# Two-layer conditioned transformer on one core: last element's stacks in layer 0's buffers, K's first half stacked ahead of Q's second, first statistics ahead of the modulation, new order tables

## The reference, cut to what matters

```python
# layer 0 (D = 256, H = 16 heads of 16)
mod = silu(cond) @ Wada + bada
sh_a, sc_a, gt_a, sh_m, sc_m, gt_m = split(mod, 6)
xm = layernorm(x, g1, be1) * (1 + sc_a) + sh_a
x  = x + gt_a * causal_attention(xm, Wqkv, Wproj, bproj)
xm = layernorm(x, g2, be2) * (1 + sc_m) + sh_m
x  = x + gt_m * (gelu(xm @ W1 + b1) @ W2 + b2)
# layer 1 (not causal; its MLP weights are not used)
h  = gamma(cond) * ln(x) + beta(cond)
q, k, v = split(h @ Wqkv1.T + bqkv1)
out = (softmax(q @ k.T) / 16) @ v
h1 = out @ Wp1.T + bp1 + x
return gamma(cond) * ln(h1) + beta(cond) + h1
```

## Time and profile before

| | us |
|---|---|
| median of 3 runs | 1286.21 (1285.28 to 1287.02) |
| the profiled execution | 1288.15 |
| its span, first to last instruction | 1286.4 |
| PE busy | 1198.2 |
| DVE busy | 858.4 |
| ACT busy | 688.6 |
| POOL busy | 273.5 |
| mean granted TensorE clock | 0.969 of 2.4 GHz |

### The profile page before, as it was taken

One profiled execution on the slowest core, in us unless ns is written; L12 is line 12 of the kernel. 1 busy time (PEld: TensorE's weight loads), 2 busy tenths in 40 slices (PEclk: granted clock), 3 DMA queues, 4 the chain that ended last, 5 costly groups with the idle time before them and its releaser, 6 DMA issues.

```text
span 1286.4 us, 18823 instructions
## 1 busy us (share of the span) xinstructions
PE 1198.2 (93%) x6604; PEld 593.7 (46%) x6604; DVE 858.4 (67%) x1779; ACT 688.6 (54%) x1356; POOL 273.5 (21%) x378
## 2 busy tenths in 40 slices
PE   6897999999999999999999999999999999999796
PEld 4434553455344644546344544446345543444223
DVE  4744478835888378855887469865797468833765
ACT  1152245465555565575555665575555666456173
POOL 1123022401133113321133113320233103220002
PEclk9789999999999999999999999999999999999698
DMA  4603022400513023410414014410414014200401
GB/s 159 199 2 99 1 67 67 125 19 18 150 37 123 2 84 85 120 39 18 128 49 134 1 63 106 105 55 19 118 56 129 2 40 104 53 26 12 105 19 42
DMA packets 59191, 89.36 MB, mean 69 GB/s; under 512 B 12914, under 2 KB 23762, under 8 KB 59098
## 3 DMA queue, kind: packets, MB, share of 16 engines
q1 hardware_dynamic: 58078, 87.35, 24.1%
q10 hardware_dynamic: 1020, 0.81, 0.2%
HBM read 24.41 MB, written 4.70 MB: 23 GB/s over the span
## 4 chain that ended last, share of the span: by engine, by line
PE 69%; ACT 9%; SPq 8%; DVE 7%; issue 3%; DMA 3%; POOL 1%; ACTq 0%; DVEq 0%; POOLq 0%
PE X L1019 17%; PE OP L927 12%; PE SC L938 10%; PE X L957 10%; PE X L1068 8%; PE X L1044 8%; ACT E L607 7%; SPq L484 6%; DVE MX L747 3%; PE X L1032 2%; DMA OC<-OE 2%; PE X L960 1%; SPq L421 1%; PE X L1097 1%; DVE XN L797 1%
## 5 line engine op out<-in xcount | busy, mean ns | idle before, releaser
L747 DVE TENSOR_REDUCE MX<-X 128x1 f32<-128x512 f32 (+3 forms) x1024 | 535.9, 585 | 182.2 <-PE X L960 111.7
L607 ACT ACTIVATE E<-SC 128x512 f32<-128x512 f32 (+3 forms) x1024 | 455.9, 527 | 340.4 <-PE SC L938 278.3
L957 PE MATMUL X<-KS,QS 96*128 96x512 bf16 (+3 forms) x1024 | 309.4, 353 | 22.6 <-DMA KS<-PART 8.9
L938 PE MATMUL SC<-QS,KS 99*128 99x512 bf16 (+3 forms) x1024 | 284.0, 347 | 21.7 <-ACT E L607 12.0
L927 PE MATMUL OP<-E,V 128*32 128x512 f32 (+3 forms) x2048 | 212.9, 533 | 4.2 <-ACT OE L622 3.1
L938 PEld LDWEIGHTS SC<-QS,KS 99*128 99x128 bf16 x1024 | 95.4, 98 | 192.0 <-ACT E L607 116.8
L957 PEld LDWEIGHTS X<-KS,QS 96*128 96x128 bf16 x1024 | 98.6, 99 | 175.3 <-DVE MX L747 59.8
L525 POOL TENSOR_SCALAR_AFFINE_SELECT E<-E 128x512 f32<-128x512 f32 x128 | 83.6, 656 | 266.7 <-ACT E L607 266.7
L1068 PE MATMUL X<-XT,W 128*128 128x512 f32 x256 | 121.9, 607 | 3.3 <-ACT XT L640 2.7
L1044 PE MATMUL X<-XT,WQKV 128*128 128x512 f32 x256 | 118.2, 605 | 1.0 <-ACT XT L640 1.0
L1019 PE MATMUL X<-W,HID 128*128 128x256 f32 x512 | 115.6, 381 | 0.5 <-ACT HID L660 0.5
(11 more groups left out here) (92 smaller groups left out, 944.0 us busy)
## 6 DMA issues: line engine op xcount, KB each, us to landing
QS<-PART SPq DMA_DIRECT2D x192, 128.0 KB, 2.3
KS<-PART SPq DMA_DIRECT2D x192, 128.0 KB, 2.4
OC<-OE SPq DMA_DIRECT2D x56, 128.0 KB, 3.8
RB<-recip_sums SPq DMA_DIRECT2D x56, 128.0 KB, 2.6
XIN<-in_x SPq DMA_DIRECT2D x8, 512.0 KB, 4.1
ROW<-row_vectors SPq DMA_DIRECT2D x8, 512.0 KB, 3.5
out<-OUT SPq DMA_DIRECT2D x7, 512.0 KB, 3.0
W<-in_w SPq DMA_DIRECT2D x2, 1024.0 KB, 7.4
```

The costliest lines, as they stand in the source:

```text
L607: a.activation(E[:, at["tick"].index() % 3, j, lo:T], SC[(at["head"].index() + j) % 3][:, lo:T], ACT.Exp, scale=HD ** -0.5 if layer == 0 e ...
L747: v.reduce_max(MX[:, qt, h:h + 1], X[at["bank"].index() % BANKS][:, 0:w], AX.X, negate=True)\
L938: t_.matmul(SC[(at["head"].index() + j) % 3][:, lo:T], KS[layer][0:ALL_ROWS, h, kt * P:kt * P + P], QS[layer][0:ALL_ROWS, h, lo:T], start= ...
L957: ins = t_.matmul(bank[:, 0:w], QS[layer][0:CUT_ROWS, h, qt * P:qt * P + P], KS[layer][0:CUT_ROWS, h, 0:w], start=True, stop=layer == 1)
```

## The change

Four edits:

- The last element's layer 1 is stacked in QS[0] and KS[0] (function `stacks`). Its stacks no longer wait for layer 1's attention of the element before but for all of layer 0's last attention (`4 * STEPS * (2 * B - 2)` exponentials). Scores, scans and the maxima's rows follow.
- A stack is issued in halves: stackq sends Q's first half (6 DMAs); stackk sends K's first half, then Q's second, then K's second.
- On DVE the first modulation (`first_modulation`) moves from ahead of the lists to inside norm_a of element 0, so behind stat_a.
- The three lists are written in another order, with the same tokens.

```diff
+def stacks(layer, b):
+    return 0 if (layer, b) == (1, B - 1) else layer
...
+            def stack(side, n, half, ready):
+                rows = slice(P // 2 * half, P // 2 * half + P // 2)
+                heads = slice(H // 2 * half, H // 2 * half + H // 2)
+                parts = (Q_PARTS, K_PARTS)[side]
+                for part in range(3):
+                    wait(sp, (high_act, cut_low, cut_low)[part], ready[part])
+                    for r in range(CUTS):
+                        if parts[r] == part:
+                            sp.dma_start((QS, KS)[side][n][r:CUT_ROWS:CUTS, heads, :],
+                                         PART[rows, side, part, :, :]).then_inc(stack_dma[n][half], 16)
...
-                    n, side = int(what[-1]), "qk".index(what[5])
+                    n, side = stacks(int(what[-1]), b), "qk".index(what[5])
                     if side == 0:
-                        wait(sp, exp_done, at["head"].at())
-                    for half in range(2):
...
+                        wait(sp, exp_done, 4 * STEPS * (2 * B - 2) if n < int(what[-1]) else at["head"].at())
+                        marks["stackq"] = marks[what[5:]]
+                        stack(0, n, 0, marks[what[5:]])
+                    else:
+                        stack(1, n, 0, marks[what[5:]])
+                        stack(0, n, 1, marks["stackq"])
+                        stack(1, n, 1, marks[what[5:]])
...
+                    if what == "norm_a" and b == 0:
+                        first_modulation()
...
-                    wait(pe, stack_dma[layer][h // (H // 2)], 192 * (b + 1))
+                    wait(pe, stack_dma[stacks(layer, b)][h // (H // 2)], 192 * (b + 1 + layer - stacks(layer, b)))
...
-    stat_a norm_a turn_a q0 stackq0 k0 mods stackk0 rows s s s s v0 s s s s s s s s s s s s s s s s s nm0_0 s s
+    stat_a norm_a turn_a q0 stackq0 k0 stackk0 mods rows s v0 s s s s s s s s s s s s s s s s s s s s s s s s s
...
-    a p a o p a p turn_1 o a t p q1 a o p a p k1 stackq1 stackk1 o v1 s s s s s s s s s s s s s s s s s s nm1_0
+    a q1 t k1 p a p stackq1 stackk1 a p a o s s p s s a s s s o s t s p s s a s p s s s a s nm1_0 p s s o row1 s
```

96 lines of the change are left out of this document (44 added, 52 removed).

## The result

| | before | after |
|---|---|---|
| median of the runs, us | 1285.99 | 1252.05 |
| lowest and highest | 1285.28 to 1287.02 | 1248.17 to 1255.32 |
| profiled execution (its span) | 1288.15 (1286.4) | 1251.06 (1249.3) |

The ratio is 0.974, with a 95% interval of 0.972 to 0.976: 34 us faster, where 16.7 were forecast.

A forecast was written before the change was run, and what follows sets the result against it. PE was taken as full mid-program, so only the late stretch and the start count: 10.8 us (last element) plus 5.9 us (opening and a wait near 203 us) make 16.7, so 1286.21 becomes 1269.5 us; range 1257 to 1284.

The forecast's parts named there:

- Part 1: Last passes: stacking the last element in layer 0's buffers, with an order that uses it, gains 10.8 us, 4 to 16.
- (a): Between turn_1's transposes and k1's end: three attention steps and two product pairs no longer stand there, 6.3 us gained.
- (b): Ahead of turn_1 in the last passes: five steps and one product pair are gone, 4 us taken, between 1 and 6.2.
- (c): From last k1's end to the last 16 steps: 26.5 us become about 24, set by ScalarE's strand; 2.5 us gained.
- the latency strand: After last k1: cuts, K's first-half DMAs, 16 maxima, then the first score; 21.2 us, shorter than ScalarE's about 24.
- (d): Among the last steps: v1's 16 matmuls now stand there and cost 3.7 us, or 0 if PE has holes.
- (e): After the late hole: the clock falls less with attention steps running through, 2 us back, 0 to 3.
- the rival in which it isn't early: Last element: SP's queue or the exponential count still holds the last stacks back, only 5.9 us left, 1280 us; chance 0.04.
- Part 2: Program start: the first statistics ahead of the modulation bring XN to 10.2 us, 2.9 us earlier, never more than 3.2.
- Part 3: Opening: K's first half ahead of Q's second gives 1.3 us at the first scan; 2.1 us near 203 us.
- Part 4: Five repeated passes in the new order: 0 us, from -1 to +2, though ten fewer table loads could give 12.8.
- VectorE ahead of turn_1: Repeated passes: seven moved maxima delay XN, each pass loses 4.2 us, 1290.5 us in all; chance 0.11.

The follow-up runs named there:

- p1: The kernel before with only the last element's layer 1 stacked in layer 0's buffers and the new order of the last passes; 1272.05 us, ratio 0.988.
- e3: The changed kernel with the old order of the opening passes put back; 1266.89 us, ratio 0.986.
- e5: The changed kernel with the new opening order only up to element 0's merge, the old opening order from there on; 1261.88 us, ratio 0.981.
- e9: The changed kernel with the old order of the repeated pass put back; 1254.76 us, ratio 0.974.
- e12: The changed kernel with the new opening order only up to just ahead of the third element's q0, the rest in old order; 1263.16 us, ratio 0.983.
- p2: The kernel before with only the first statistics put ahead of the first modulation; 1285.28 us, ratio 0.999.
- e6: The changed kernel with the first modulation again ahead of the first statistics; 1257.22 us, ratio 0.979.
- p3: The kernel before with only the stacks issued by halves, all orders old; 1280.67 us, ratio 0.997.
- e7: The changed kernel with whole stacks again, 12 DMAs of Q and then 12 of K; 1264.29 us, ratio 0.982.
- e10: The kernel before with the exponentials between element 1's eight gelus moved out, four table loads fewer; 1287.57 us, ratio 1.001.

## Why the prediction was wrong, point by point

**The direction was right, and the two places that were costed gave about what was forecast. The sum was half, because what lay between them was put at nothing.** In the order of its steps:

*Part 1, the last element: right, a little small.* 10.8 forecast; S6 gives 13.1, and 11.4 with part 1 alone. By its terms, from the Q stack that starts S6 to k1's end 135.3 us became 123.4, so (a) and (b) are 11.9 for 10. From k1's end to the first of the last 16 steps 26.5 became 25.6, so (c) is 0.9 for 2.5, and it was costed on the wrong strand. ScalarE's, my 24 us, holds only 16.8 us of work in the 25.6 (and its terms add up to 22.4 to 22.9, not to 24). What lasted was the latency strand, 21.2 in the prediction: 8.2 us to the first scan where 6.4 were counted (K's first half is issued after 5.1 us and not 4.0, and PE is in a product with V until 8.2), 10.5 from there to the end of the 16th maximum, and 6.9 to the first score where 5.2 were, with one more product with V just ahead of it. From there to the end 70.55 became 70.26, so (d) and (e) are +0.3 for -1.7. Either v1's 3.6 us fit into PE's idle time, which is 14.7 us there before and 14.1 after, or the clock, 0.91 before and 0.95 after, gave back more than the 2 counted; no run parts the two. The early stack is real: Q's DMAs start at 1150.79 with eight steps of the element before still to come, so the rival in which it isn't early is dead. The 13.1 is rather low. In e3, e5, e9 and e12, which run the same instructions there, S6 is 216.2 to 217.0 us with the clock at 0.98, against 219.3 and 0.96.

How big the prize could be was weighed with the Trainium skill ("Perfetto Trace Analysis", Identifying the Most-Contended Engine, on weight loads as the better measure than matmul busy time). The 7.2 us of the earlier trace rows and the 13.1 of S6 don't test this: the first is PE's idle time in one stretch of 32 us, and in all of S6 it was 30.6 us and became 21.5. The hole itself gave little, 11.9 us of the 13.1 lie ahead of k1's end. The trace agrees with the page in S5: PE's busy time falls by 12.0 us between e9 and the kernel after, while the weight loads' stays, at 356.3 and 356.8, and so does the time, at 726.4 and 726.0.

Two side sums of the prediction are off, and nothing rests on them. The prediction's 1275 with 7.2 as the whole prize doesn't come out by putting 7.2 for the 10.8, which gives 1273.1; it takes v1's 3.7 and the clock's 2 on top. And ScalarE's 39 us of the 52 in the last steps leave 13, not 12.

*Part 2, the statistics: right.* XN at 9.95 for 10.2, S1 2.5 to 4.3 us shorter for 2.9 (p2 and after against e6).

*Part 3, the halves: right in place, small in one term, and 2.1 us too large in another.* First scan 31.90 for 32.5, maxima from 37.47 for 38.5, v0 not slowed. The first score is at 53.58 instead of 58.65, 5.1 us earlier for 3.8. The wait for K's stack in S4 is gone, as forecast, but it was not worth its 2.1 us: with the halves and the old order S4 is 137.0 to 137.6, with the wait 137.6 to 139.7, 138.3 in the kernel before. The halves' value at the end, 3.5 us by p3 and e7, was inside the reckoning of (c).

*What followed the opening: the step that failed.* The prediction took the first list as two places: the opening, worth 3.8 us, and "one more place, near 203 us, where PE waits 2.1 us for K's stack". Everything else between the first score, at 58.65 us, and the end of S4, at 323.58, was put at nothing. The traces show 5.1 us gained by the first score and 19.5 by the end of S4, so 14.5 us where 2.1 were counted: 4.9 in what is left of S2, 2.4 in S3 and 7.2 in S4. The list's 461 tokens run to 324 us, and the order of all that stands behind element 0's merge was changed too. I costed it at that one wait because the stretch of the earlier trace rows at 544 us has PE at 32.00 of 32, and I took what holds for the repeated pass for the passes ahead of it. A busy row of 185 to 324 us would have shown 6.8 us idle of 138 and the four kinds of waits.

What is shown of the cause differs by stretch. In S4 it is the order, worth 6 to 7 us (e5, and all 17 kernels of the table). S3 is 2 to 4 us shorter in most kernels with the new order, but part of its work has moved ahead of the mark; e5 keeps S3 at 79.4 with the old order behind the merge. S2's 4.9 go for the most part with the clock, as told below. By which mechanism the order shortens S4 is open: not the table loads (e10), not the wait for K's stack. The 7.2 us are 3.8 of idle time and 3.4 of shorter rows of PE, but S5 shows that the time need not follow either: there 12.0 us of rows and 16 us of waits change with the order, and the time stands.

*The clock: counted as 2 us, about 8 go with it.* Each run comes with its mean granted clock. Within the runs of one kernel, 171 runs in 20 groups, each taken against its group's mean, 0.01 of clock goes with 9.0 us (standard error 0.5). The kernel before has 0.974 (68 runs), the one after 0.983 (4 runs): 0.009 x 900 = 8 us. Most of it lies in S2 (0.83 before, 0.91 after) and S6 (0.93 and 0.96). These 8 us are no addition to the stretches, they are a part of them, and they are a correlation: no kernel here set the clock alone, and which brings the other is not shown.

*Part 4, the repeated pass: right.* 0 forecast, 145.2 us a pass where 146.1 were, and e9, with 145.3, gives no sign that even this is the order's. The table loads, from 51 to 41, are worth nothing, in e9 as in e10. VectorE ahead of turn_1 didn't become the bound. The low end of the range was drawn from those table loads, the one thing in the change that is worth nothing, so it was short by 5 us for a reason that had nothing to do with the loads.

**S2 stays partly open.** Its length goes with its clock. p1 has the instructions of the kernel before there. The rows of S2 in the kernel before, in p1 and in the kernel after:

```profile
22.76:103.21 80.45, 70.83 (x435) 35.80 (x433) 44.16 (x106) 30.27 (x77) 19.25 (x35) 0.83 0.32 100
```

```profile
23.45:99.69 76.24, 65.92 (x435) 35.31 (x433) 43.36 (x106) 29.83 (x77) 19.25 (x35) 0.91 0.33 105
```

```profile
19.66:93.25 73.59, 64.38 (x443) 34.34 (x441) 42.80 (x106) 30.44 (x77) 16.84 (x34) 0.91 0.35 109
```

So of the 6.9 us some 4.2 go with the clock and are within what chance does to the same instructions, and 2.6 are left for the edits at the same clock, with eight matmuls more in them. The new order with the halves has 73.6 to 73.9 at 0.91 (four kernels) and 77.0 and 77.1 at 0.87 (e6 and e5), the new order with whole stacks 79.6 at 0.87 and 82.8 at 0.84, and the old order 76.2 to 83.1. Four kernels at 0.91 can hardly be chance alone, but e5 has their instructions and not their clock. These are single executions, and what sets the clock there was not found.
